# Last layer of a four-layer transformer stack: its weights split in the attention before it, its first products issued ahead of the gates in eight PSUM banks, its result stored batch by batch

## The reference, cut to what matters

```python
def _L3_ffn_ref(x, A_w, B_w, Wq_w, keys):    # RANK 8, 64 experts, TOP_K 16, ROUTER_DIM 16, SCALING 2
    q = jnp.einsum('bsd,rd->bsr', x, Wq_w)
    scores = jnp.einsum('bsr,er->bse', q, keys)
    top_vals, top_idx = jax.lax.top_k(scores, TOP_K)
    top_w = jax.nn.softmax(top_vals, axis=-1)
    gate = jnp.sum(jax.nn.one_hot(top_idx, NUM_EXPERTS, dtype=top_w.dtype) * top_w[..., None], axis=-2)
    z = jnp.einsum('bsd,nd->bsn', x, A_w)                      # 512 x 512: first factor
    z_gated = (z.reshape(..., 64, 8) * gate[..., None]).reshape(..., 512)
    return jnp.einsum('bsn,on->bso', z_gated, B_w) * SCALING   # 512 x 512: second factor
```

## Time and profile before

| | |
|---|---|
| median of 3 runs | 3027.27 us (3024.07 to 3029.74) |
| profiled execution, own time | 3025.75 us |
| its span, first to last instruction | 3023.6 us |
| mean granted TensorE clock | 0.971 of full |
| busy share of the span: PE, PEld, DVE, ACT, POOL | 94%, 81%, 66%, 47%, 44% |
| f3, from its first norm instruction to its last add | 2922.8 to 3014.0 us |
| store, from issue to landing | 7.2 us |

### The profile page before, as it was taken

How to read it: one execution, slowest core, us unless ns; L and a number is a source line. 1 busy time by engine, 2 the same in 40 slices (tenths; PEclk the granted TensorE clock), 3 DMA queues, 4 the chain that set the end, 5 groups by cost and what they waited for, 6 DMA issues and landing times. The chain is left out here.

```text
span 3023.6 us, 44597 instructions
## 1 busy us (share of the span) xinstructions
PE 2829.5 (94%) x16196; PEld 2451.1 (81%) x16196; DVE 2007.0 (66%) x3531; ACT 1429.4 (47%) x3473; POOL 1326.2 (44%) x1180
## 2 busy tenths in 40 slices
PE   7999999999986996999999999988999999999977
PEld 6888888888874884778888877868999899898865
DVE  5787778877765778789999974344454444545453
ACT  3666656566631673144454433215545545455530
POOL 6455545545421754565555530013434434444430
PEclk9999999999987997999999999999999999999988
DMA  3121212212121002111111103100001000000000
GB/s 131 52 67 55 59 56 66 66 48 63 44 84 44 15 5 70 39 43 43 42 43 43 33 21 123 42 22 22 29 18 29 29 19 29 26 28 22 18 29 28
DMA packets 77816, 131.85 MB, mean 44 GB/s; under 512 B 10016, under 2 KB 23584, under 8 KB 77216
## 3 DMA queue, kind: packets, MB, share of 16 engines
q1 hardware_dynamic: 68096, 112.09, 12.3%
q10 hardware_dynamic: 9504, 16.91, 1.7%
HBM read 114.23 MB, written 14.75 MB: 43 GB/s over the span
## 5 line engine op out<-in xcount | busy, mean ns | idle before, releaser
L89 PE MATMUL a_pa<-a_wo,a_ot 128*128 128x512 f32 x2304 | 536.6, 391 | 13.0 <-issue 9.3
L89 PEld LDWEIGHTS a_pa<-a_wo,a_ot 128*128 128x128 f32 x2304 | 430.0, 188 | 106.9 <-issue 18.4
L356 DVE SCALAR_TENSOR_TENSOR a_nf_acc<-a_nf_t,a_nf_acc 128x512 f32<-128x512 bf16 (+1 forms) x462 | 401.9, 870 | 35.2 <-ACT a_nf_t L309 4.9
L89 PE MATMUL a_pa<-h_t,a_wqk 128*128 128x512 f32 x1536 | 372.6, 395 | 1.7 <-DVE h_t L769 1.7
L309 ACT ACTIVATE a_nf_t<-a_nf_w,a_nf_shifts 128x512 bf16<-128x512 f32 (+1 forms) x495 | 321.1, 709 | 59.0 <-DVE a_nf_acc L356 33.7
L89 PEld LDWEIGHTS a_pa<-h_t,a_wqk 128*128 128x128 f32 x1536 | 281.8, 188 | 55.8 <-DVE h_t L769 1.9
L89 PE MATMUL a_pa<-a_wv,ctx_t 128*128 128x512 f32 x960 | 232.3, 398 | 30.7 <-POOL a_wv L526 16.7
L89 PEld LDWEIGHTS a_pa<-a_wv,ctx_t 128*128 128x128 f32 x960 | 180.3, 191 | 68.0 <-issue 16.7
L89 PE MATMUL a_pa<-ctx_t,a_wqk 128*128 128x512 f32 x960 | 224.8, 390 | 2.5 <-POOL a_wqk L1679 2.2
L1010 POOL TENSOR_TENSOR a_prob<-a_prob,a_inv 128x512 f32<-128x512 f32 x128 | 132.5, 1057 | 210.8 <-DVE a_inv L1391 210.8
L89 PEld LDWEIGHTS a_pa<-ctx_t,a_wqk 128*128 128x128 f32 x960 | 179.7, 188 | 41.3 <-POOL a_wqk L1679 4.2
(11 more groups left out here) (363 smaller groups left out, 6114.2 us busy)
## 6 DMA issues: line engine op xcount, KB each, us to landing
a_raw<-in_a_w SPq DMA_DIRECT2D x288, 256.0 KB, 2.6
a_nf_w<-in_nf ACTq DMA_DIRECT2D x32, 256.0 KB, 2.7
nf_rounded<-a_nf_acc ACTq DMA_DIRECT2D x32, 256.0 KB, 2.0
f_rows<-nf_rounded SPq DMA_DIRECT2D x22, 256.0 KB, 3.1
ctx_kept<-ctx_t SPq DMA_DIRECT2D x1, 4096.0 KB, 16.5
ctx_t<-ctx_kept SPq DMA_DIRECT2D x1, 4096.0 KB, 15.0
f_cols<-nf_rounded SPq DMA_DIRECT2D x11, 256.0 KB, 3.9
a_ctx_raw<-in_ctxt SPq DMA_DIRECT2D x4, 512.0 KB, 7.6
```

The lines of the kernel that those rows point to most:

```text
L89: ins = nc.tensor.matmul(out, lhs(a), rhs(b), start=first and i == 0, stop=last and i == 2)
L356: ins = nc.vector.scalar_tensor_tensor(acc, t, c, acc, inner, outer)
```

## The change

1. a3 gets the loads and most splits of f3's weights. SP loads the first factor once the last key/value product is made, router and keys, and the second factor once the first 28 heads are weighed. GpSimd splits the first factor in four pieces of 128x512: two behind head 29's work, two and the router's and keys' splits behind head 30's, so ahead of `split(("o", 31))`.
2. f3 uses all eight banks as a ring: each batch's bank takes the first product, then the transposed, then the second product. The norm's transposes use banks 4 to 7, the router's products 4 and 5, the scores 6.
3. TensorE's order: first products 0 to 2 between the norm's last transposes, 3 and 4 around the second router product, 5 to 7 behind the scores; then transposes of b+1 ahead of the second product of b. Only the second factor is split in f3 (GpSimd).
4. Gates: ScalarE is freed for the exponentials after the first maxima; mask and multiply are one instruction; the factor 2 goes into the last one.
5. VectorE in the loop: gating of b+2, rest of b+1, add of b.
6. SP stores each batch (256 KB) when added; the store stage and its barrier go.

```diff
@@ latent_attention_stage, sync @@
+            sp.wait_ge(a_ready, made_count["kv", KV_HEADS - 1, 3, 1])
+            sp.dma_start(f3["raw_a"][:, :, :], a_in.rearrange("(c p) n -> p c n", p=P)).then_inc(a_loaded, 16)
+            sp.wait_ge(ks_ready, 4 * KV_HEADS)
...
+            sp.dma_start(f3["raw_k"][:, :], keys_in).then_inc(small_loaded, 16)
+            sp.wait_ge(o_ready, 2 * (H - 4))
+            sp.dma_start(f3["raw_b"][:, :, :], b_in.rearrange("(c p) n -> p c n", p=P)).then_inc(b_loaded, 16)
@@ latent_attention_stage, gpsimd @@
+            def prefetch_a(c):
+                if c == 0:
+                    pool.wait_ge(s_ready, 4 * (H - 4))
+                    pool.wait_ge(a_loaded, 16)
+                nc.gpsimd.tensor_scalar(f3["wa"][:, HI, c, :], f3["raw_a"][:, c, :], 1.0, 0.0, ALU.mult, ALU.add
+                                        ).then_inc(a_hi, 1)
+                pool.wait_ge(a_hi, c + 1)
+                nc.gpsimd.tensor_tensor(f3["wa"][:, LO, c, :], f3["raw_a"][:, c, :], f3["wa"][:, HI, c, :].bitcast(F32),
+                                        ALU.subtract).then_inc(low_done, 1)
+
+            def prefetch_small():
+                pool.wait_ge(small_loaded, 32)
+                for n, (w, raw_w) in enumerate(((f3["router"], f3["raw_r"]), (f3["keys"], f3["raw_k"]))):
+                    nc.gpsimd.tensor_scalar(w[:, HI], raw_w[:], 1.0, 0.0, ALU.mult, ALU.add).then_inc(small_hi, 1)
+                    pool.wait_ge(small_hi, n + 1)
+                    nc.gpsimd.tensor_tensor(w[:, LO], raw_w[:], w[:, HI].bitcast(F32), ALU.subtract).then_inc(low_done, 1)
...
+                if h == H - 3:
+                    prefetch_a(0)
+                    prefetch_a(1)
+                elif h == H - 2:
+                    prefetch_a(2)
+                    prefetch_a(3)
+                    prefetch_small()
@@ ffn3_stage @@
+    Z_BANK = (0, 1, 2, 3, 7, 4, 5, 6)
+    S_BANK = 6
...
+            for b in range(NB):
+                sp.wait_ge(x_done, b + 1)
+                sp.dma_start(out[b, :, :], x[:, b, :]).then_inc(stored, 16)
+            sp.wait_ge(stored, 16 * NB)
...
+            for b in range(4):
+                norm.transposes(pe, b)
+            for b in range(4, NB):
+                norm.transposes(pe, b)
+                if b < 7:
+                    low(b - 4)
+            route(0)
+            low(3)
+            route(1)
+            low(4)
+            scores()
+            low(5)
+            low(6)
+            low(7)
+            pe.wait_ge(b_split, 2)
+            turned(0)
+            for b in range(NB):
+                if b + 1 < NB:
+                    turned(b + 1)
+                outputs(b)
...
+            dve.wait_ge(best_ready, NB)
+            nc.vector.tensor_scalar(shift[:, :], best[:, :, 0], -1.0, None, ALU.mult).then_inc(shift_ready, 1)
...
-            steps.mark(nc.vector.tensor_scalar(left[:, :, :], left2[:, :, :], TAKEN, None, ALU.is_equal))
+            dve.wait_ge(exp_done, NB)
+            steps.mark(nc.vector.scalar_tensor_tensor(left[:, :, :], left2[:, :, :], TAKEN, e[:, :, :], ALU.is_equal, ALU.mult))
...
             gated(0)
             gated(1)
+            rest_of_turned(0)
             for b in range(NB):
...
                 if b + 2 < NB:
                     gated(b + 2)
+                if b + 1 < NB:
+                    rest_of_turned(b + 1)
                 dve.wait_ge(o_ready, b + 1)
```

More of the change, by code:

```diff
@@ L198, in on_tensor @@
     def on_tensor(self, pe):
         for b in range(NB):
[L200 to L205, removed]
+            self.transposes(pe, b)
         pe.wait_ge(self.lo_done, NB)
@@ L860 @@
 LATENT_RING = 4
+E3, R3, RD3 = 64, 8, 16
 KV_HEADS = 8
@@ new lines, in ffn3_stage, with at @@
+def ffn3_stage(nc, x, ident, h_t, free_at, weights, carried, out):
+    st = Stage(nc, "f3")
+    KB = 1024
+    wa, raw_b, router, keys = (weights[n] for n in ("wa", "raw_b", "router", "keys"))
+    def at(offset, name, shape, dt=F32):
+        return nc.alloc_sbuf_tensor_at(f"f3_{name}", shape, dt, offset=free_at + offset)
+    wb = at(16 * KB, "wb", [P, 2, DC, D], F32R)
+    zg = at(40 * KB, "zg", [P, 2, D])
+    zt = at(44 * KB, "zt", [P, 2, 2, DC, P], F32R)
+    q = at(52 * KB, "q", [RD3, 2, NT], F32R)
+    s, left, left2, e = (at((84 + 2 * i) * KB, n, [P, NB, E3]) for i, n in enumerate(("s", "left", "left2", "e")))
+    best = at(92 * KB, "best", [P, NB, 16])
+    shift, total, inv = (at(92 * KB + 512 + 32 * i, n, [P, NB]) for i, n in enumerate(("shift", "total", "inv")))
+    bank = st.ps("bank", [P, 8, BANK])
+    (own, b_split, q_ready, q_hi, q_lo, s_ready, s_copied, best_ready, shift_ready, exp_done,
+     z_ready, z_used, tr_ready, tr_hi, tr_used, o_ready, x_done, stored) = (st.sem(n) for n in (
+         "own b_split q_ready q_hi q_lo s_ready s_copied best_ready shift_ready exp_done "
+         "z_ready z_used tr_ready tr_hi tr_used o_ready x_done stored").split())
+    Z_BANK = (0, 1, 2, 3, 7, 4, 5, 6)
+    S_BANK = 6
+    norm = TransposedNorm(nc, st, carried, x, ident, h_t, [bank[:, n, :] for n in range(4, 8)],
+                          at(68 * KB, "norm_h", [P, NB, D]))
@@ L3146, in _ @@
             pool.wait_ge(norm.h_ready, NB)
[L3147 to L3152, removed]
+            nc.gpsimd.tensor_scalar(wb[:, HI, :, :], raw_b[:, :, :], 1.0, 0.0, ALU.mult, ALU.add).then_inc(b_split, 1)
@@ L3154, in _, with low @@
+            pool.wait_ge(b_split, 1)
+            nc.gpsimd.tensor_tensor(wb[:, LO, :, :], raw_b[:, :, :], wb[:, HI, :, :].bitcast(F32),
+                                    ALU.subtract).then_inc(b_split, 1)
         @block.tensor
         def _(pe):
[L3156 to L3160, removed]
-                for c in range(DC):
-                    ins = mm3(nc, pq[0:RD3, :], lambda p: router[:, p, c, :],
+            def low(b):
+                pe.wait_ge(norm.lo_done, NB if b == 4 else b + 1)
+                if b in (5, 6):
+                    pe.wait_ge(q_lo, b - 4)
+                if b == 7:
+                    pe.wait_ge(s_copied, 1)
+                for c in range(DC):
+                    ins = mm3(nc, bank[:, Z_BANK[b], :], lambda p: h_t[:, p, c, b * P:(b + 1) * P],
+                              lambda p: wa[:, p, c, :], c == 0, c == DC - 1)
+                ins.then_inc(z_ready, 1)
@@ L3163, in _, with route @@
+            def route(half):
+                pe.wait_ge(norm.lo_done, (5, NB)[half])
+                for c in range(DC):
+                    ins = mm3(nc, bank[0:RD3, 4 + half, :], lambda p: router[:, p, c, :],
                               lambda p: h_t[:, p, c, half * BANK:(half + 1) * BANK], c == 0, c == DC - 1)
                 ins.then_inc(q_ready, 1)
-            pe.wait_ge(q_lo, 2)
-            for b in range(NB):
-                ins = mm3(nc, ps_[:, b * E3:(b + 1) * E3], lambda p: q[:, p, b * P:(b + 1) * P], lambda p: keys[:, p, :])
```

198 lines of the change are left out of this document (80 added, 118 removed).

## The result

The changed kernel takes 2997.47 us (median of 4 runs, 2996.1 to 2999.82), the kernel before 3026.03 in the same timing: ratio 0.9903, 95% interval 0.989 to 0.9915, 28.6 us less. A second timing gave 2999.29 against 3025.99: 0.9908, 0.9892 to 0.9924, 26.7 less. The forecast was 3002.5, 24.8 less, in a range from 2997 to 3009. The direction, the place and the mechanism came out as forecast; the gain was larger.

What follows compares the result with a forecast made beforehand. TensorE's holes in the last layer, its slow clock and the final 2 MB store were taken as the bounds. 2990.7 + 2.9 + 1.8 + 3.4 = 2998.8 against 3023.6: 24.8 us less, median 3002.5, range 2997 to 3009.

Steps and rivals of the forecast that it cites:

- (b): f3's start to the scores: TensorE waits for nothing after the fifth transposes; scores done at 2952.8, 0.6 us later than before.
- (a): Tail of a3: splits ahead of wo's split for head 31 make TensorE wait 2.9 us more (2.3 to 3.1).
- (c): Gates: copy of the scores to first gating takes 9.7 us instead of 12.36; first gated batch at 2962.5.
- (d): First output: 2.01 us from transposes to products; outputs start at 2964.6, the second factor's split done by 2938.
- (e): Output loop: TensorE sets the pace, 3.25 us per batch; last add ends at 2990.7.
- R4: Rival, output loop: each output waits for its own transposes and rest; period 4.8 us, +11, 3013; chance 0.07.
- (f): Store: 3.4 us behind the last add instead of 9.57, the last 256 KB landing in 2.0 (bounds 2.0 and 7.2).
- (g): TensorE's clock: one fall, in a3's hole or before the first output, at 1.8 us; bounds none and three.
- R2: Rival, a3: no stall and no clock fall, 2998 us; chance 0.12.
- R5: Rival, f3: TensorE's clock stays at 1.2 GHz, 18 products slow, +42 us, 3043; chance 0.03.
- R3: Rival: three clock falls (a3's stall, start, gates) or a late last store, 3006 to 3010 us; chance 0.19.
- R6: Rival, f3: old holes merely moved, 3012 us, or all gain eaten, no change; chance 0.04.

Runs made afterwards that it cites:

- e1: Changed kernel with all four first-factor pieces and the small splits behind head 29's work: stretch 94.46 and 97.36 us (changed 98.85), ratio 0.9898 to the kernel before.
- e3: Changed kernel with the gates in their old order and with their old instructions: stretch 104.89 us, 6.0 more than changed.
- e2: Changed kernel with one 2 MB store behind the last add instead of eight of 256 KB: stretch 104.13 us, 5.3 more than changed.
- e6: Changed kernel with the scores behind three first products instead of five: stretch 94.44 us, 4.4 less than changed.
- e4: Changed kernel, eight banks kept, with first products in their old places: none before the scores; stretch 107.80 us, 9.0 more than changed.
- e8: e7 with the 24 small score products mixed with one first product's 12: stretch 93.85 and 94.84 us, ratio 0.9891 to the kernel before.
- e7: Changed kernel with the edits of both e1 and e6: stretch 95.40 us, 3.4 less than changed.

## Why the prediction was right or wrong

The forecast stretch is 125.1 - 24.8 = 100.3 us; 98.7 and 99.0 were measured. What failed is the size of a term, not the mechanism: term (b), which took "norm and transposes 0 to 4 as before" and counted the router products at their length behind a hole. Step by step:

- **(a) Wait in a3.** Right in place and releaser: 2.42 us idle and 2.66 of delay, forecast 2.9 (2.3 to 3.1). The four small splits took 1.2 us together, not 1.4. e1 shows the cause by moving the splits away.
- **(b) To the scores.** No hole between the fifth transposes and the scores, as forecast, but the largest missed size: 29.1 us from the norm's start to the copy, forecast 30.1 (the 29.5 of the kernel before and 0.6). TensorE reached its first product 5.3 us after the norm's start, forecast 5.8; the clock was at 0.50 there for under 4 us instead of over 6. The two router products took 2.87 and 2.78 us from start to start, where the sum has 2.96 each, the length of one that stood alone behind a hole. The first of these is partly luck: with a long slow stretch in the norm again (e1's second profile) the same part took 30.5.
- **(c) Gates.** 9.56, forecast 9.7. The fused instructions cost 0.69, like plain ones, not 0.75. e3 shows that the removed 2.8 us were all on the path.
- **(d) First output.** 2.2 us, forecast 2.1.
- **(e) Output loop.** 25.7 us, forecast 26.1; products 3.21 apart, not 3.25. TensorE sets the pace; R4 falls.
- **(f) Store.** 3.5 behind the last add, forecast 3.4; landing 2.0. e2 shows it.
- **(g) Clock.** One fall at 1.8 beside the norm's was put into the sum. One paid fall is there, behind the wait in a3 (1.6: 12.76 less 11.17). A second, behind the scores, cost almost nothing: the products under the gates took 10.04 and ended 0.4 behind the gating, as (c) had said of this case. The place was left open in the forecast, between a3's hole and the gates'. That the count of paid falls came out as one is luck: e6 and e4 had none behind the same wait in a3.

Against the forecast, (b) gave 1.0 us, (a) and the paid fall together 0.4, (e) 0.4 and (c) 0.1; (d) and (f) cost 0.1 each: 1.6 us in the first profile.

The forecast median missed by 5.0 us (3002.5 against 2997.47). Of these 1.6 are the terms above. 1.2 are the kernel before, whose median in the same timing was 3026.03 and not the 3027.27 that the forecast started from. The other 2.2 lie outside the stretch; the two profiles show 2.9 of this kind ahead of the change. They are scatter: the second timing has 1.9 us less of gain. The range was made of the terms' bounds only and held nothing for this scatter, so its lower end of 2997 is too high: single executions took 2995.54 and 2996.1.

R2 (no wait) and R5 fell: the clock was at 1.00 for 24.9 busy us of 25 in the output loop with eight banks in turn, so what the Trainium skill, TensorE: Matmul & The Clock Gate, section "A second HAM failure mode: psum-queue depth-cycling", describes does not show here. R3 fell too: of the two falls beside the norm's only one was paid, and the last store landed in 2.0. R6 fell by the changed profile itself, in which the old holes are filled and not moved; e4 adds that 9.0 us hang on the order.

What is open: what decides whether a slow stretch follows a hole of 2.4 us. With the same wait in a3 it came in four profiles (changed twice, e2, e3) and not in two (e4, e6). Open also: what the eight banks by themselves give, and VectorE's new order in the loop; no run takes them back alone.

## What to carry to other kernels

Work moved early into another engine's queue is judged by what stands behind it there: here 5 us of splits put ahead of one needed instruction cost 4.25 us, and the same splits one head earlier left the part up to the norm as it was before. A store issued per piece leaves only the last piece behind the last add. For changes of a few us in a long kernel compare a stretch that begins at an instruction which both kernels have, and take it twice. It repeated to 0.25 us in both kernels where the time ahead of it moved by 3.7, but by 1.0 in e8 and 2.9 in e1, where the slow clock fell differently. And a lone instruction's length is too long for a sum of instructions that follow each other without a hole: 2.96 against 2.8 here.

## What the runs showed of the hardware that was not expected

TensorE can be busy all the time and still be granted less. In the changed kernel it was busy in every us from 2930 to 2953 at a clock of 1.00, and then, behind 24 matmuls of 16x64, the clock was 0.50 from 2954 to 2956; the same happened in the second profile of the changed kernel and in e1, e2 and e3. Mixed with large matmuls it stayed at 1.00 twice, but unmixed it did so too in three of twelve profiles, so the small matmuls are a suspect and not a shown cause. One program had its slow stretches at different places and of different length from one execution to the next: e1 took 70.1 and 73.0 us from norm to end, and the f3 that e6 and e7 share took 67.3 and 71.0.
